# A routed feed-forward layer whose results are scattered to the tokens instead of fetched by index, in three groups of chunks instead of four

## What is computed

```python
logits = xf @ Wg
topw, topi = jax.lax.top_k(logits, 2)
topw = jax.nn.softmax(topw, axis=-1)
gu = jnp.einsum('nd,edh->enh', xf, Wgu) + bgu[:, None, :]
g, u = jnp.split(gu, 2, axis=-1)
eo = jnp.einsum('enh,ehd->end', jax.nn.silu(g) * u, Wd) + bd[:, None, :]
out = jnp.einsum('end,ne->nd', eo, comb)     # comb: topw at topi, 0 elsewhere
h = h + _L0_attn_ref(_layernorm(h))          # and then
h = h + out                                   # with xf = _layernorm(h)
```

## Time and profile before

| | |
|---|---|
| median of 3 runs | 820.52 us (817.84 to 821.28) |
| the profiled execution | 824.18 us, span in the trace 822.4 us |
| mean granted clock of TensorE | 0.84 of full |
| busy, share of the span | PE 73%, POOL 61%, DVE 52%, ACT 32% |
| share of the chain that ended last | PE 37%, POOL 21%, DVE 14%, issue 13%, DMA 7% |

### The profile page before, as it was taken

One profiled execution on the slowest core, in us unless ns is written; L12 is line 12 of the kernel. 1 busy time (PEld: TensorE's weight loads), 2 busy tenths in 40 slices (PEclk: granted clock), 3 DMA queues, 4 the chain that ended last, 5 costly groups with the idle time before them and its releaser, 6 DMA issues.

```text
span 822.4 us, 12791 instructions
## 1 busy us (share of the span) xinstructions
PE 603.9 (73%) x3335; PEld 519.1 (63%) x3335; DVE 430.1 (52%) x1708; ACT 264.7 (32%) x690; POOL 498.1 (61%) x520
## 2 busy tenths in 40 slices
PE   3787645327778788698989986999898969999000
PEld 2687634316567576586878875888787758888000
DVE  4789655343556657265655766355544623445122
ACT  2502122112234432244442543254253324444000
POOL 5602327763655756377677776477777767760674
PEclk9998855557789988698997997899999979999555
DMA  7185000126345533565655663667577768984221
GB/s 152 53 290 148 1 0 26 33 90 186 101 127 153 145 104 106 164 194 150 185 169 154 205 198 106 191 202 218 179 214 235 236 197 257 279 279 147 80 77 61
DMA packets 84597, 125.23 MB, mean 152 GB/s; under 512 B 15044, under 2 KB 57792, under 8 KB 84526
## 3 DMA queue, kind: packets, MB, share of 16 engines
q1 hardware_dynamic: 72526, 101.66, 40.9%
q0 software_dynamic: 11520, 22.35, 9.5%
q10 hardware_dynamic: 480, 0.41, 0.4%
HBM read 84.25 MB, written 43.25 MB: 155 GB/s over the span
## 4 chain that ended last, share of the span: by engine, by line
PE 37%; POOL 21%; DVE 14%; issue 13%; DMA 7%; ACT 3%; SPq 3%; POOLq 0%; DVEq 0%; ACTq 0%
PE gu L587 15%; PE dn L587 11%; POOL gat L1048 8%; POOL xbuf L1034 8%; PE mx L587 5%; POOL rs L966 3%; DMA gat<-ybuf,ypos 3%; PE xTp L765 3%; DMA space<-xbuf 2%; DMA space<-in_x_dram 2%; PE tr L587 2%; ACT x L894 1%; PE tr L719 1%; DVE gat L1485 1%; DVE rec L1268 1%
## 5 line engine op out<-in xcount | busy, mean ns | idle before, releaser
L1034 POOL DMA_INDIRECT xbuf<-x,pos x180 | 186.4, 1035 | 112.9 <-DVE pos L1369 56.0
L587 PE MATMUL gu<-space,wts 128*128 128x256 f32 x912 | 246.0, 410 | 9.1 <-DVE space L1476 9.1
L1476 DVE SCALAR_TENSOR_TENSOR space<-gu,wts,space 128x256 f32<-128x256 f32 x228 | 109.1, 482 | 235.7 <-ACT space L912 173.3
L1048 POOL DMA_INDIRECT gat<-ybuf,ypos x180 | 177.7, 987 | 87.9 <-issue 55.5
L912 ACT ACTIVATE space<-gu,wts 128x256 f32<-128x256 f32 x228 | 109.1, 479 | 305.7 <-PE gu L587 305.3
L587 PEld LDWEIGHTS gu<-space,wts 128*128 128x128 f32 x912 | 174.8, 206 | 32.0 <-DVE space L1476 10.9
L587 PEld LDWEIGHTS dn<-wts,space 128*128 128x128 f32 x912 | 127.9, 204 | 14.1 <-DVE space L1476 7.1
L587 PE MATMUL dn<-wts,space 128*128 128x128 f32 x912 | 129.1, 288 | 5.8 <-DVE space L1476 5.8
L765 PE MATMUL xTp<-cst,space 128*128 128x128 f32 x228 | 51.8, 311 | 40.2 <-DMA space<-xbuf 38.1
L765 PEld LDWEIGHTS xTp<-cst,space 128*128 128x128 f32 x228 | 26.7, 154 | 52.6 <-DMA space<-xbuf 40.8
L966 POOL TENSOR_TENSOR rs<-ve,nhalf 128x4 f32<-128x4 f32 (+2 forms) x39 | 40.4, 1036 | 29.7 <-DVE ve L1281 15.2
(11 more groups left out here) (198 smaller groups left out, 837.8 us busy)
## 6 DMA issues: line engine op xcount, KB each, us to landing
wts<-wall SPq DMA_DIRECT2D x114, 386.0 KB
space<-xbuf SPq DMA_DIRECT2D x114, 128.0 KB, 2.6
ybuf<-space SPq DMA_DIRECT2D x114, 128.0 KB
xbuf<-zero_rows SPq DMA_DIRECT2D x4, 1024.0 KB, 10.5
xt<-in_txt_dram SPq DMA_DIRECT2D x16, 256.0 KB, 3.0
xbuf<-zero_rows SPq DMA_DIRECT2D x32, 128.0 KB
out_dram<-gat SPq DMA_DIRECT2D x16, 256.0 KB
xbuf<-x,pos POOLq DMA_INDIRECT x180
```

What stands on the lines that cost most here:

```text
L587: return nc.tensor.matmul(o, l, r, start=a, stop=z_)
L1034: nc.gpsimd.indirect_dma_start(out=xbuf, out_offset=bass.IndirectOffsetOnAxis(pos[0:p, c:c + 1], 0), in_=x2[n % NX2][0:p, m // 2 * D:(m // ...
L1048: nc.gpsimd.indirect_dma_start(out=gat[b][0:p, (k * W4 + j) * D:(k * W4 + j + 1) * D], out_offset=None, in_=ybuf[g], in_offset=bass.Indire ...
L1476: V.scalar_tensor_tensor(hid[q % 4], gu_ps[q % 3][:, SLOT:2 * SLOT], wts[k % NW][:, W_B + HT + t:W_B + HT + t + 1], sil[q % 3], ALU.add, A ...
```

## The change

Each token row carries two more numbers now (`ROW = D + 2`): the weight of this expert and the number of the row where its result belongs. `x2` holds the chunk twice, for its two experts (ACT's `x_copy`, and `meta` written by DVE), and the scatter takes rows of 130 numbers. ACT scales each result row by the weight that came with it, in two operations a tile, and POOL scatters the tile's 256 rows to `results`, two indirect transfers a tile, at the place that came with them. The store to `ybuf`, the fetches by index, `ypos` and `places_of_results` go. SP loads a chunk's results with one plain transfer (`load_results`), DVE adds the two of a token and the token's row, and SP stores. `text_y` moves from POOL to DVE. Rows that stand for no token need a place too, in a spare part of `results`, so that POOL numbers them in `zero_rows` before they are written. The groups end at chunks 4, 13 and 23 with 20, 40 and 47 tiles, together 107.

```diff
-GROUPS = [(0, 4), (4, 11), (11, 18), (18, 23)]
+GROUPS = [(0, 4), (4, 13), (13, 23)]
...
-NX = 5
+NX = 7
...
-NG = 4
+NG = 3
...
+ROW = D + 2
...
@@ SP
             load_images(1)
-            sp.wait_ge(W.zero_ok, 1)
+            sp.wait_ge(W.spare_ok, 1)
             for g in range(len(GROUPS)):
                 sp.dma_start(xbuf[ROW0[g] + E * CAP[g]:ROW0[g + 1], :].rearrange("(e p s) d -> p e (s d)", e=E, s=SUB),
-                             zero_rows[:, :].unsqueeze(1).to_broadcast([P, E, SUB * D])).then_inc(W.spare, 16)
+                             zero_rows[:, :].rearrange("p (e c) -> p e c", e=E)).then_inc(W.spare, 16)
...
-                wait(sp, W.xTt_ok, k - NX + 1)
...
+                if k >= NX:
+                    sp.wait_ge(yrow_out[(k - NX) % NYB], stored_before(k - NX))
+                sp.dma_start(xrow[k % NX], xbuf[bass.ds(row, SLOT), :].rearrange("(p s) d -> p (s d)", s=SUB)
+                             ).then_inc(xrow_in[k % NX], 16)
...
+            def load_results(n):
+                b, g, p = n % NG, group_of(n), parts(n)
+                if n == GROUPS[g][0]:
+                    for m in range(TILE0[g + 1] - NYB, TILE0[g + 1]):
+                        sp.wait_ge(yrow_out[m % NYB], stored_before(m))
+                wait(sp, W.sum_ok, n - NG + 1)
+                r0 = n * A_CHUNK
+                sp.dma_start(res[b][0:p, 0:2 * width(n) * D].rearrange("p (j c) -> p j c", j=width(n)),
+                             results[r0:r0 + p * 2 * W4, :].rearrange("(p j k) d -> p j (k d)", p=p, k=2)[:, 0:width(n)]
+                             ).then_inc(res_in[b], 16)
...
@@ ACT
+            def x_copy(n):
+                p, w = parts(n), width(n)
+                act.wait_ge(W.x2_ok, n + 1)
+                rows = x2[n % NX2][0:p, :].rearrange("p (k j c) -> p k j c", k=2, j=W4)
+                copy(rows[:, 1, 0:w, 0:D], rows[:, 0, 0:w, 0:D]).then_inc(W.copy_ok, 1)
...
-                copy(yrow[k % NYB], dn_ps[k % 2][:, 0:SUB * D]).then_inc(W.y_row_ok, 1)
+                for s in range(SUB):
+                    last = nc.scalar.activation(yrow[k % NYB][:, s * D:(s + 1) * D], dn_ps[k % 2][:, s * D:(s + 1) * D], ACT.Copy,
+                                                scale=xrow[k % NX][:, s * ROW + D:s * ROW + D + 1])
+                last.then_inc(W.y_row_ok, 1)
...
@@ POOL
             def scatter(n, m):
...
                 if m == 0:
                     pool.wait_ge(W.pos_ok, n + 1)
-                    pool.wait_ge(W.x2_ok, n + 1)
+                    pool.wait_ge(W.meta_ok, n + 1)
+                    pool.wait_ge(W.w1_ok, n + 1)
+                if m == 1:
+                    pool.wait_ge(W.copy_ok, n + 1)
...
-            def gather(n, j, k):
...
+            def scatter_rows(k):
+                pool.wait_ge(W.y_row_ok, k + 1)
+                for s in range(SUB):
+                    place = xrow[k % NX][:, s * ROW + D + 1:s * ROW + D + 2].bitcast(I32)
+                    nc.gpsimd.indirect_dma_start(out=results, out_offset=bass.IndirectOffsetOnAxis(place, 0),
+                                                 in_=yrow[k % NYB][:, s * D:(s + 1) * D], in_offset=None
+                                                 ).then_inc(yrow_out[k % NYB], 16)
+
+            def number_pads(base):
+                ids = zero_rows[:, :].bitcast(I32).rearrange("p (e s c) -> p e s c", e=E, s=SUB)[:, :, :, D + 1]
+                return nc.gpsimd.iota(ids, [[SLOT, E], [1, SUB]], base=base, channel_multiplier=SUB)
+
+            pool.wait_ge(W.zero_ok, 1)
+            pool.wait_ge(W.seen_zero, 2)
+            number_pads(SPARE_ROW).then_inc(W.spare_ok, 1)
+            pool.wait_ge(W.spare, 16 * len(GROUPS))
+            number_pads(PAD_ROW).then_inc(W.pads_ok, 1)
             for i in range(FIRST, ITERS):
...
+                    for k, t in units(i, s):
+                        if t == 1:
+                            if k >= 2 and not any(first_of_group(m) for m in range(k - 1, k + 1)):
+                                scatter_rows(k - 2)
...
@@ DVE, weights
+                dve.wait_ge(W.x2_ok, n + 1)
+                V.tensor_scalar(meta[:, :, 0:w, D + 1].bitcast(I32), place0[0:p, :].rearrange("p (k j) -> p k j", k=2)[:, :, 0:w],
+                                n * A_CHUNK, None, ALU.add).then_inc(W.meta_ok, 1)
...
@@ DVE, combine
-                for j in range(w):
-                    last = V.scalar_tensor_tensor(rows[1][j], rows[1][j], wn[1][j], h1_of(n)[0:p, j * D:(j + 1) * D], ALU.mult, ALU.add)
...
+                V.tensor_tensor(rows[:, :, 0], rows[:, :, 0], rows[:, :, 1], ALU.add).then_inc(W.half_ok, 1)
                 dve.wait_ge(W.half_ok, n + 1)
...
+                V.tensor_tensor(h, h, rows[:, :, 0], ALU.add).then_inc(W.sum_ok, 1)
```

More of the change, by code:

```diff
@@ L74 @@
 QUAD = 4
-GROUP_POS = max(b - a for a, b in GROUPS) * W4 * 2
 def tile_group(k):
@@ L183, in opens, with loads @@
     return OPENS_AT.get(i * SLOTS + s, [])
-def gathers(i, s):
-    return GATHERS_AT.get(i * SLOTS + s, [])
+def loads(i, s):
+    return LOADS_AT.get(i * SLOTS + s, [])
 def combines(i, s):
@@ L214, in program @@
     bias2 = nc.dram_tensor("bias2", (E, 2, SUB * D), F32, kind="Internal").ap()
-    xbuf = nc.dram_tensor("xbuf", (ROW0[-1], D), F32, kind="Internal").ap()
-    ybuf = [nc.dram_tensor(f"ybuf{g}", (KT[g] * SLOT, D), F32, kind="Internal").ap() for g in range(len(GROUPS))]
+    xbuf = nc.dram_tensor("xbuf", (ROW0[-1], ROW), F32, kind="Internal").ap()
+    results = nc.dram_tensor("results", (RESULT_ROWS, D), F32, kind="Internal").ap()
     with ctx:
@@ L279, in program @@
         top[0] = 6 * ROWS
-        xrow = [part(SUB * D) for _ in range(NX)]
+        xrow = [part(SUB * ROW) for _ in range(NX)]
         xT = [part(SLOT) for _ in range(2)]
@@ L303, in program @@
         yT = sb("yT", [P, W4 * D])
-        x2 = [sb(f"x2{i}", [P, W4 * D]) for i in range(NX2)]
+        x2 = [sb(f"x2{i}", [P, 2 * W4 * ROW]) for i in range(NX2)]
         x2T = sb("x2T", [P, W4 * D])
@@ L387, in program @@
         yrow_out = [sem(f"s_yrow_out{i}") for i in range(NYB)]
-        gat_in = [sem(f"s_gat_in{i}") for i in range(NG)]
-        gat_out = [sem(f"s_gat_out{i}") for i in range(NG)]
+        res_in = [sem(f"s_res_in{i}") for i in range(NG)]
         sent = [sem(f"s_sent{i}") for i in range(NX2)]
@@ L425, in stored_before, with loaded_before @@
         def stored_before(k):
-            return 16 * (k // NYB + 1)
-        def gathered_before(n):
-            return 16 * sum(2 * width(m) for m in range(n % NG, n + 1, NG))
-        def out_before(n):
-            return 16 * sum(width(m) if m < IMG_CHUNKS else 1 for m in range(n % NG, n + 1, NG))
+            return 16 * SUB * (k // NYB + 1)
+        def loaded_before(n):
+            return 16 * (n // NG + 1)
         @block.sync
@@ L518, in pad @@
                     skip_runtime_bounds_check_because=inside)[1]
-                for row in rows:
-                    sp.dma_start(xbuf[bass.ds(row, SLOT), :].rearrange("(p s) d -> p s d", s=SUB),
-                                 zero_rows[:, :].rearrange("p (s d) -> p s d", s=SUB)).then_inc(W.padded, 16)
+                sp.wait_ge(W.pads_ok, 1)
+                for e, row in enumerate(rows):
+                    sp.dma_start(xbuf[bass.ds(row, SLOT), :].rearrange("(p s) d -> p (s d)", s=SUB),
+                                 zero_rows[:, e * SUB * ROW:(e + 1) * SUB * ROW]).then_inc(W.padded, 16)
             def load_tile(k):
@@ L564, in _ @@
                                 load_tile(k + AHEAD)
-                        else:
-                            if k >= 2 and not any(first_of_group(m) for m in range(k - 1, k + 1)):
-                                store_tile(k - 2)
-                            if last_of_group(k):
-                                store_tile(k - 1)
-                                store_tile(k)
                     if due("text_load", i, s):
@@ L577, in _ @@
                         store_out(n)
+                    for n in loads(i, s):
+                        load_results(n)
                     for g in opens(i, s):
@@ L580, in _ @@
                             load_tile(TILE0[g] + k)
-            for m in range(CHUNKS - NG, CHUNKS):
-                sp.wait_ge(gat_out[m % NG], out_before(m))
+            sp.wait_ge(W.out, 16 * sum(1 if n >= IMG_CHUNKS else width(n) for n in range(CHUNKS)))
         @block.tensor
@@ L1018, in gate_exp @@
                 tt(ex[0:p, 0:w], euler[0:p, 0:w], gap[0:p, 0:w], ALU.pow).then_inc(W.ex_ok, 1)
-            def text_y(n):
-                b = n - IMG_CHUNKS
-                pool.wait_ge(W.cum_ok, b + 1)
-                wait(pool, W.mix_ok, n if b > 0 else 0)
-                tt(yT[:, :], cum[:, :], pow_t[:, REV + T_IMG:REV + T], ALU.mult).then_inc(W.y_ok, 1)
             def scatter(n, m):
@@ L1062, in _ @@
                         scatter(i, SCATTER_SLOTS.index(s))
-                    for n, j, k in gathers(i, s):
-                        gather(n, j, k)
```

(11 more changed lines are left out.)

138 lines of the change are left out of this document (47 added, 91 removed).

## The result

The changed kernel takes 866.0 us in the median of four runs (861.59 to 867.74), the kernel before 820.9 beside it (817.84 to 824.05): a ratio of 1.054, 95% interval 1.049 to 1.059. It is slower, and 865 was forecast.

The account below looks back on a forecast made before the run. PE and POOL queues nearly full in the middle, PE in the last group, POOL's gathers in the tail. +15 seam, +3.5 weights, -17 middle, +66 last tiles, -22 tail: +45 us, about 865 us, range 835 to 895.

Parts of the forecast that it names:

- the last group: Final tiles, nothing beside them: 47 in place of 27 at 3.30 us each, 160.4 us in all, +66 us.
- the middle: From chunk 4's placing to the last group's first tile: POOL becomes the bound, 455.4 us against 472.6, -17 us.
- slack: Time per middle chunk beyond the fuller queue's work: 1.5 us, with bounds 0 and 3.
- Rival 1: Middle follows PE, at under 0.95 us an indirect transfer: 372 us in place of 455, whole 782 us; chance 0.06.
- The 3.5 us for chunks 0 to 3: Scatter 0 waits for the weights on DVE, 0.9 us a chunk with nothing hiding it: +3.5 us.
- The seam: After the image products, POOL numbers spare rows and waits for SP's three writes: +15 us (10 to 18).
- The splitting of ACT's copy: Last group: two scaled copies of 0.41 us against one of 0.38, costing nothing while PE keeps 3.3 us.
- rival 3: Last group: tile buffers return late; slower scatters and loads would make 3.9 us a tile, +28 us, 893; chance 0.13.
- The tail: After PE's end: 40 gathers go, last scatters, loads, sums and stores remain, 39 us (34 to 47), -22 us.
- DVE beside POOL: DVE's two-input operations against POOL's transfers: a few us gain by the row, no loss by the rule; sum unchanged.
- Rival 2: The middle loses its 1.5 us of slack a chunk (27 us): 838 us, 834 with a 12 us seam; chance 0.15.

## Why the prediction was right, and where it was off

**The sign and the size** were right, and for chunks 13 to 21 and the last group by the mechanism named: in the middle two scatters for each tile stand on POOL behind every tile, and the tiles that left the middle for the last group cost 3.30 us each where nothing runs beside them. The sum of the terms was 8 us too high; that 865 met 866.0 so closely is in part luck: the changed kernel's profiled execution lies 4.4 us under its median, and 3.7 had been taken off for that of before.

**The middle**, 455.4 forecast and 456.9 measured. The two times met, place(13) at 412 (414.5) and place(22) at 640 (634.8), hide errors that cancel. The loop began 4.3 us earlier than forecast, and from there place(4) to place(13) took 206.2 us, not 199.4, and place(13) to place(22) 220.3, not 228. In chunks 4 to 11 POOL's sum was right (18.9 a chunk, forecast 19.1), but its waits for DVE made the slack 2.8 us a chunk, not 1.5. In chunks 13 to 21 the sum was too high: 144 transfers were counted, 134 are in the trace, and they cost 1.32 us, not 1.30, busy and gap together. That "every pair in the trace shows 1.255 to 1.30" held for the stretches that were read; in chunks 11 to 16 of before, fetches take 1064 ns in the mean and 9.2 us of gaps for 27 of them, 1.40 us each.

That POOL binds chunks 13 to 21 is shown from four sides: its sum is 92% of the stretch and 97% with the weights early; halving the scatters (with the weights early) takes 33.6 of the 55.6 us off there; cutting PE's work takes nothing; and with fetches POOL's queue is 29.7 us shorter and the stretch 37.1. Before chunk 13 the same halving takes 13 us off for 20 scatters, but the queue is not full, and what binds these chunks is open. Rival 1's 372 us is near what the middle becomes with half of the result scatters (384.9), and its turning point, 0.95 us a transfer, was not met: 980 to 1016 ns busy and about 0.3 of issue.

**A row was read too kindly.** That w is ready "0.5 us after pos at 127.08" was true of chunk 0, where no tile runs. With tiles beside it w came 3.6 us after pos in chunk 15, and the middle pays 16.4 us for the slot (0.86 a chunk). The sum did not show it, because the 1.5 us of slack a chunk was taken whole and an interval of 25.3 us holds such a wait: the forecast chunk of 13 to 21 was 25.3, the measured 24.5, of which 22.5 are the queue. The 3.5 us for chunks 0 to 3 were 4.2.

**The seam** was mis-sized, 15 for 12 (from the end of the image products at 112.99 to rs at 125.00); the 10.0 of the table has 2.0 us of an earlier image stage in it. The three writes took 2.54 us to issue and 7.4 to land (median), where the four of before took 7.59 and 10.5.

**The last group** met its forecast of 160.4 us: (820.75 - 678.07)/43 is 3.32 us a tile, most of them 3.30. The splitting of ACT's copy cost nothing. What was wrong is the room given to rival 3: "a tile may be 2.4 us" stands against some 3.2 measured. The loads of a tile's rows landed after 3.2 us in the median (2.0 to 5.0, in the last group), not 2.2, which is 1 of the some 3 us that the loop is longer; the rest was not taken apart.

**The tail** was 34.1 us, forecast 39 (34 to 47). The 4 us of last scatters were 5.1 (825.7 to 830.8), the first loads were issued 1.4 us after them and not 2, and loads and stores came to 27.6 us (832.2 to 859.8) where 28 + 5 were given: the ends overlap with the transfers.

By the Trainium skill's page "DMA: Bandwidth & Descriptors", section "Anatomy of one DMA", the estimate for a load of 512 KB was 3.2 us; the page fits it on transfers that GpSimd issues, and these are SyncE's. In this trace the first sum starts 3.6 us after the issue of the first load (832.20 to 835.84), with two more loads behind it: roughly so. How 34 us for the tail follow from it is not worked out, so that 34.1 was measured speaks for the page only weakly.

**DVE beside POOL.** Text_y on DVE gains about 1%. Scatters of results take 1016 ns in chunks 13 to 21 and fetches 1002 in chunks 18 to 21 of before, 1064 in chunks 11 to 16: no loss that could be told. The Trainium skill's page "SBUF — State Buffer" ("Who interferes with whom") would let DVE's operations with two SBUF inputs hold up POOL's reads. The changed kernel's result scatters do take longer beside a busier DVE (1016 ns at 49%, 969 in the last group at 35%), but no run takes the page's rule apart from the other load of these stretches.

**Rival 2** (the slack lost, 838 us) was not met. The weights' slot was 16.4 of the 27 us called slack: with it changed, 848.9, still 11 above.
